# A small transformer on one core: the encoder's residual goes from identity products on TensorE to rows added by VectorE, and maxima products are spread between feed-forward products

## The reference

```python
def layer(h, p):                       # 6 times, on h = x + pos_encoding
    q, k, v = (h @ w + b, split into 16 heads of 8)
    scores = einsum("bhqd,bhkd->bhqk", q, k) / sqrt(8)
    scores = scores * sierpinski_mask
    att = softmax(scores) @ v, merged heads, @ wo + bo
    h = _ln(h + att, g1, be1)
    ff = gelu(h @ w1 + b1) @ w2 + b2   # 128 -> 512 -> 128
    return _ln(h + ff, g2, be2)
```

## Time and profile before

| what | value |
|---|---|
| time, median of 3 runs | 4445.66 us (4441.06 to 4448.02) |
| the profiled execution's time | 4436.53 us |
| its span, first to last instruction | 4434.5 us |
| TensorE busy | 3725.7 us (84%) |
| VectorE busy | 2560.0 us (58%) |
| ScalarE busy | 1880.3 us (42%) |
| GpSimd busy | 783.7 us (18%) |
| mean granted TensorE clock | 0.916 |

### The profile page before, as it was taken

How to read it: one execution, slowest core, us unless ns; L and a number is a source line. 1 busy time by engine, 2 the same in 40 slices (tenths; PEclk the granted TensorE clock), 3 DMA queues, 4 the chain that set the end, 5 groups by cost and what they waited for, 6 DMA issues and landing times. The chain is left out here.

```text
span 4434.5 us, 72029 instructions
## 1 busy us (share of the span) xinstructions
PE 3725.7 (84%) x27991; PEld 2608.3 (59%) x27991; DVE 2560.0 (58%) x6629; ACT 1880.3 (42%) x2957; POOL 783.7 (18%) x1073
## 2 busy tenths in 40 slices
PE   5998998998998998995999987677756666997996
PEld 3766666676666766764777754465635432443664
DVE  4756756756756756755222229888678572113763
ACT  2554564654654654653333335322223122331443
POOL 2223212212222222222000001000010230003321
PEclk8999999999999999997999998799877677997997
DMA  5424414414414514511000000000000000002430
GB/s 130 116 46 106 115 41 111 115 36 118 114 37 113 121 37 104 125 33 44 1 1 1 1 15 1 1 1 1 1 6 1 4 0 27 0 0 75 99 88 24
DMA packets 156743, 222.66 MB, mean 50 GB/s; under 512 B 16158, under 2 KB 136350, under 8 KB 139422
## 3 DMA queue, kind: packets, MB, share of 16 engines
q10 hardware_dynamic: 19656, 107.37, 10.9%
q1 hardware_dynamic: 136750, 110.69, 9.1%
HBM read 154.42 MB, written 60.82 MB: 49 GB/s over the span
## 5 line engine op out<-in xcount | busy, mean ns | idle before, releaser
L755 DVE TENSOR_REDUCE enc_mx<-psum 128x2 f32<-128x512 f32 (+1 forms) x1152 | 750.8, 684 | 261.5 <-PE psum L464 259.4
L900 ACT ACTIVATE enc_e<-psum 128x1024 f32<-128x1024 f32 (+1 forms) x768 | 580.3, 808 | 376.1 <-PE psum L483 309.2
L464 PE MATMUL psum<-enc_ks,enc_qs 80*128 80x128 bf16 (+1 forms) x3072 | 453.5, 252 | 88.6 <-DVE enc_mx L755 71.9
L483 PE MATMUL psum<-enc_qs,enc_ks 83*128 83x256 bf16 (+1 forms) x3072 | 378.4, 248 | 18.9 <-DMA enc_qs<-enc_turned_max 13.3
L464 PEld LDWEIGHTS psum<-enc_ks,enc_qs 80*128 80x128 bf16 x3072 | 216.9, 99 | 223.2 <-DVE enc_mx L755 129.0
L494 PE MATMUL psum<-enc_e,enc_v 128*32 128x256 f32 (+1 forms) x6144 | 329.3, 332 | 0.0
L1775 ACT ACTIVATE moe_act_h<-psum 128x512 f32<-128x512 f32 x288 | 169.4, 598 | 306.8 <-PE psum L1649 306.7
L483 PEld LDWEIGHTS psum<-enc_qs,enc_ks 83*128 83x128 bf16 x3072 | 258.1, 98 | 55.0 <-DMA enc_qs<-enc_turned_max 17.9
L1671 PEld LDWEIGHTS psum<-par_s,moe_act_h 128*128 128x128 f32 x2304 | 269.7, 192 | 30.1 <-issue 28.5
L1671 PE MATMUL psum<-par_s,moe_act_h 128*128 128x128 f32 x2304 | 272.6, 275 | 0.0
L1738 DVE SCALAR_TENSOR_TENSOR moe_acc<-psum,moe_gates,moe_acc 128x128 f32<-128x128 f32 x256 | 72.1, 344 | 345.3 <-PE psum L1671 345.3
(11 more groups left out here) (468 smaller groups left out, 7183.9 us busy)
## 6 DMA issues: line engine op xcount, KB each, us to landing
enc_qs<-q_pieces ACTq DMA_DIRECT2D x234, 192.0 KB
enc_ks<-k_pieces ACTq DMA_DIRECT2D x234, 192.0 KB
k_pieces<-enc_pieces SPq DMA_DIRECT2D x240, 128.0 KB, 2.0
q_pieces<-enc_pieces SPq DMA_DIRECT2D x144, 128.0 KB, 2.1
enc_qs<-q_pieces SPq DMA_DIRECT2D x54, 192.0 KB
enc_ks<-k_pieces SPq DMA_DIRECT2D x54, 192.0 KB
rope_qs<-q_pieces ACTq DMA_DIRECT2D x39, 192.0 KB
rope_ks<-k_pieces ACTq DMA_DIRECT2D x39, 192.0 KB
```

What stands on the lines that cost most here:

```text
L464: last = T_.matmul(p1[f % 2][:, i * kw:(i + 1) * kw], qs[0:KEYED, slot, h, j * P:(j + 1) * P], ks[0:KEYED, slot, h, 0:kw], start=True, sto ...
L483: last = T_.matmul(p2[ch][:, g], ks[0:SCORED, slot, 4 * T + g, ch * P:(ch + 1) * P], qs[0:SCORED, slot, 4 * T + g, 0:n], start=True, stop= ...
L755: V.tensor_reduce(mx[:, u % 2, j * HEADS + h0:j * HEADS + h0 + n], p1[f % 2].rearrange("p (h k) -> p h k", h=n), AX_X, ALU.max)\
L900: A.activation(e_of(T, ch), p2[ch], ACT.Exp, scale=HD ** -0.5).then_inc(s_e, 1)
```

## The change

1. The residual is kept as rows. `res` (one slot for each of the 8 groups) holds what is to be added. After N1's apply of a group GpSimd writes `res = normed * g1 + (be1 + b2)` for the feed-forward (`residual1`, two instructions, L376 and L379 of the kernel after), and after N2's apply `res = normed * g2 + (be2 + bo of the next layer)` for the next layer's attention (`residual2`, L384 and L387). `shifts` makes the two sums of biases once in a layer.
2. VectorE adds `res` to the rows in PSUM and writes `rows` (`add1`, L817, and `add2`, L826), in place of ScalarE's `move`. The identity products, `held` and `hold` are gone.
3. Gains and biases are now wanted as rows on all partitions: `layerr` grows from 128x1162 to 128x1928 words, the constants `s1` by 128 columns. SyncE waits for `residual2` of the last group (`s_res2`) before it loads the next `layerr`.
4. At the start TensorE turns the 8 groups of `H` into rows (32 transposes) and VectorE makes the first `res` with 8 adds.
5. The maxima products of the next layer are put one by one behind each `up` product and behind each tile of `down` from g = 5 on; the last six come after the loop.

```diff
@@ sync, attend
                     sp.wait_ge(N2.s_done, at(layer, GROUPS, 2 * GROUPS))
+                    sp.wait_ge(s_res2, at(layer, GROUPS, 2 * GROUPS))
                     sp.dma_start(LR.sb[:], c.params["layerr"][1:][ds(layer, 1)].rearrange("l p w -> p (l w)")).then_inc(LR.sem, 16)
@@ gpsimd
-            def hold(layer, half, g):
...
-                G.tensor_tensor(held[:, half, g % 2], c.H[:, grp(g)], bias.broadcast_to([P, GROUP]), ALU.add).then_inc(s_held[half], 1)
+            def residual2(layer, g):
+                n = at(layer, GROUPS, g)
+                pool.wait_ge(N2.s_normed, n + 1)
+                G.tensor_tensor(res[:, g], N2.normed[:], LR["g2r"].unsqueeze(1).broadcast_to([P, TILES, D]), ALU.mult).then_inc(s_scaled2, 1)
+                pool.wait_ge(s_scaled2, n + 1)
+                pool.wait_ge(s_shift2, layer + 1)
+                G.tensor_tensor(res[:, g], res[:, g], shift2[:].unsqueeze(1).broadcast_to([P, TILES, D]), ALU.add).then_inc(s_res2, 1)
@@ gpsimd, attend
-                        if m:
-                            hold(layer, 0, m - 1)
+                        if m == 1:
+                            shifts(layer, last)
+                        if m >= 2:
+                            residual1(layer, m - 2)
+                        if u == 0 and layer:
+                            residual2(layer - 1, GROUPS - 1)
...
                 for g in range(GROUPS):
+                    if g >= 2 and not last:
+                        residual2(layer, g - 2)
                     if g:
                         N2.root(pool, at(layer, GROUPS, g - 1))
@@ tensor
-                    T_.matmul(b[:, sl], att_t[:, sl], LR["wo"], start=True, stop=False)
-                    last = T_.matmul(b[:, sl], held[:, 0, g % 2, sl], c.ident, start=False, stop=True)
+                    last = T_.matmul(b[:, sl], att_t[:, sl], LR["wo"], start=True, stop=True)
...
-                    T_.matmul(down_bank[:, sl], held[:, 1, g % 2, sl], c.ident, start=True, stop=False)
...
+                    between(t)
@@ tensor, attend, feed-forward
+                    behind = (lambda f: fill(layer, 1, (g - 5) // 2, 6 * ((g - 5) % 2) + f) if f < 3 else None) if g >= 5 and not last_layer else (lambda f: None)
                     if g + 1 < GROUPS:
-                        up(layer, g + 1)
+                        up(layer, g + 1, behind)
...
-                    down(layer, g)
+                    down(layer, g, among)
@@ vector
+            def add1(layer, g, b):
+                n = at(layer, GROUPS, g)
+                dve.wait_ge(N1.s_rows, n + 1)
+                dve.wait_ge(s_res2, n + 1)
+                if n:
+                    dve.wait_ge(N1.s_normed, n)
+                V.tensor_tensor(N1.rows[:], b.rearrange("p (t d) -> p t d", t=TILES), res[:, g], ALU.add).then_inc(N1.s_moved, 1)
@@ vector, attend
+                        if T == 0 and odd and m:
+                            add1(layer, m - 1, misc)
...
+                    if n and not last:
+                        dve.wait_ge(s_scaled2, n)
...
                     N2.apply(dve, n)
+                    if 1 < g < GROUPS:
+                        add2(layer, g)
```

More of the change, by code:

```diff
@@ L425, in attend @@
                 N2.root(pool, at(layer, GROUPS, GROUPS - 1))
+                if not last:
+                    residual2(layer, GROUPS - 2)
                 if last:
@@ L476, in scores_t @@
                 slot = u % SLOTS
+                if layer == 0 and u == 0 and T == 0 and ch == 0:
+                    pe.wait_ge(s_res2, GROUPS)
                 if T == 0 and ch == 0:
@@ L538, in up, with down @@
                     T_.matmul(up_bank[f], LR["w1"][:, f * P:(f + 1) * P], c.H[:, grp(g)], start=True, stop=True).then_inc(s_h, 1)
-            def down(layer, g):
-                pe.wait_ge(s_held[1], at(layer, GROUPS, g + 1))
+                    between(f)
+            def down(layer, g, between=lambda t: None):
                 if g:
@@ L656, in attend @@
                 for g in range(GROUPS):
+                    behind = (lambda f: fill(layer, 1, (g - 5) // 2, 6 * ((g - 5) % 2) + f) if f < 3 else None) if g >= 5 and not last_layer else (lambda f: None)
                     if g + 1 < GROUPS:
-                        up(layer, g + 1)
+                        up(layer, g + 1, behind)
+                    else:
+                        for f in range(3):
+                            behind(f)
                     if g == 0:
@@ L698, in attend @@
                         close(g)
-                    if 4 <= g and not last_layer:
-                        u, f0 = ((0, 0), (0, 6), (1, 0), (1, 6))[g - 4]
-                        for f in range(f0, f0 + 3):
-                            fill(layer, 1, u, f)
                 if not last_layer:
-                    for f in range(9, 12):
+                    for f in range(6, 12):
                         fill(layer, 1, 1, f)
@@ L721, in _ @@
             project_v(0, 0, 0, bank[0])
+            for g in range(GROUPS):
+                if g >= len(x_banks):
+                    pe.wait_ge(s_res2, g - len(x_banks) + 1)
+                for t in range(TILES):
+                    last = T_.transpose(x_banks[g % len(x_banks)][:, t * P:(t + 1) * P], c.H[:, g * GROUP + t * P:g * GROUP + (t + 1) * P], c.ident)
+                last.then_inc(s_x_rows, 1)
             for u in range(2):
@@ L782, in normalise, with add2 @@
                 V.tensor_tensor(out, num[:, half, :, :, 1:VW], rec[:, half].unsqueeze(3).broadcast_to([P, JT, hh, HD]), ALU.mult).then_inc(s_att, 1)
+            def add1(layer, g, b):
+                n = at(layer, GROUPS, g)
+                dve.wait_ge(N1.s_rows, n + 1)
[3 more added lines that the diff above has]
+                V.tensor_tensor(N1.rows[:], b.rearrange("p (t d) -> p t d", t=TILES), res[:, g], ALU.add).then_inc(N1.s_moved, 1)
+            def add2(layer, g):
+                n = at(layer, GROUPS, g)
+                dve.wait_ge(N2.s_rows, n + 1)
+                dve.wait_ge(s_res1, n + 1)
+                if n:
+                    dve.wait_ge(N2.s_normed, n)
+                V.tensor_tensor(N2.rows[:], down_bank.rearrange("p (t d) -> p t d", t=TILES), res[:, g], ALU.add).then_inc(N2.s_moved, 1)
             def close(k):
@@ L833, in attend @@
                         dve.wait_ge(N2.s_turned, n)
+                    if g == 1:
+                        add2(layer, 0)
                     N2.statistics(dve, n)
                     if g == 1:
+                        add1(layer, GROUPS - 1, bank[1])
                         N1.statistics(dve, at(layer, GROUPS, GROUPS - 1))
@@ L869, in _ @@
             move_v(0, 0, 0, bank[0])
+            for g in range(GROUPS):
+                dve.wait_ge(s_x_rows, g + 1)
+                V.tensor_tensor(res[:, g], x_banks[g % len(x_banks)].rearrange("p (t d) -> p t d", t=TILES),
+                                W["bo0"].unsqueeze(1).broadcast_to([P, TILES, D]), ALU.add).then_inc(s_res2, 1)
             for u in range(2):
@@ L952, in attend @@
                                 act.wait_ge(LR.sem, at(layer, 16, 16))
-                            N1.move(act, at(layer, GROUPS, m - 1), misc)
                         if T == 0 and u:
@@ L975, in attend @@
                         move_att(layer, GROUPS - 1, bank[0])
-                    if g == 1:
-                        N1.move(act, at(layer, GROUPS, GROUPS - 1), bank[1])
                     if g == 3 and not last:
```

69 lines of the change are left out of this document (39 added, 30 removed).

## The result

| | before | changed |
|---|---|---|
| time, median (lowest to highest) | 4446.84 us (4439.24 to 4449.69, 6 runs) | 4428.14 us (4422.73 to 4434.6, 6 runs) |
| ratio to before, 95% interval | | 0.9961 [0.995, 0.9973] |
| profiled execution; its span | 4436.53 us; 4434.5 us | 4428.41 us; 4426.6 us |

The change made the kernel 18.7 us faster (0.4%). The forecast was 58 us faster, and 4428.14 lies just above the upper end of its range.

What follows compares the result with a forecast made beforehand. TensorE was taken to bound attention nearly everywhere, feed-forward less surely. Terms 37 + 45 + 4 - 25 - 3 - 1.5 = 56.5, say 57 us, took the profiled 4436.5 to 4380; 9 us offset gave 4388 us, range 4358 to 4428.

Steps and rivals of the forecast that it cites:

- rival 1: Whole kernel: the gains and losses come as summed, 4388 us, own range 4368 to 4408; chance 0.62.
- Groups 0 to 2: 3.6 us: Feed-forward, not last layer: three down and one set of attention rows save 0.89 us each, 3.6 us a layer.
- Of 0.89 + 1.97 us I keep 0.8: Feed-forward group 4: identity saving and held wait go, but root ends 1.7 us later; 0.8 us a layer gained.
- rival 5: Attention: GpSimd's longer work holds up VectorE's normalising, 2.5 us for each of 42 pairs, 105 us, 4493 us; chance 0.04.
- Groups 5 and 6 and the tail: Feed-forward: groups 5 and 6 gain 2.0 us in all, group 7 and tail 2.5 us (1 to 3), a layer.
- TensorE has a block of value products and a maxima product to do before it wants bank 5 again, which covers it: Attention: VectorE's new add costs nothing; without cover it would cost 42 x 0.75 = 32 us.
- Rival 3: Attention gives nothing back, as VectorE's maxima come late behind the attention rows: + 37, 4425 us; chance 0.08.
- in a stretch without a gap on TensorE: Attention: 7 of 8 groups' rows are made where TensorE never idles, so removing identity products saves 37 us.
- forecast's split: Layer boundary: TensorE's 4.9 us wait for the row of maxima, 3.5 us without the load ahead in the queue.
- 3 us for five boundaries: Layer boundaries: after the new wait the granted clock can be 0.50 for a stretch; 3 us lost (0 to 9).
- The start's term: Kernel start: larger layerr and constants are issued ahead of the bit rows, 1.5 us lost; transposes and adds cost nothing.
- Rival 4: Feed-forward: gain from spacing the maxima products is lost in turn's new wait, 4 us a layer less, 4408 us; chance 0.14.

Runs made afterwards that it cites:

- Experiment 6: experiment 1 with GpSimd's residual1 of group 7 moved ahead of root of group 1 in the feed-forward; 4379.26 us, ratio 0.9864 to before.
- Experiment 7: experiment 1 with residual2 of group 2 between the pieces of groups 0 and 1, and of group 6 ahead of the last root; 4381.76 us.
- experiment 8: experiment 1 with the moves of Experiment 5, Experiment 6 and Experiment 7 together; 4360.55 us, ratio 0.9822 to before.
- experiment 1: The changed kernel with the last group's residual2 issued at the layer's end, not behind the next layer's pieces; 4390.13 us, ratio 0.9893 to before.
- Experiment 5: experiment 1 with VectorE's add1 in odd sequences placed before its second block of maxima, not after; 4377.46 us, ratio 0.9862 to before.
- experiment 2: The changed kernel with SyncE issuing the row of maxima of sequence 1 ahead of the layerr load; 4419.67 us, ratio 0.9952 to before.
- experiment 4: The kernel of before with only the spreading of the feed-forward's maxima products, identity products kept; 4423.55 us, ratio 0.9959 to before.
- Experiments 3: The changed kernel with the feed-forward's maxima products back in blocks of three, so the residual part alone; 4445.05 us, ratio 1.0012 to before.

## Why the prediction was wrong

The mechanisms were those forecast in rival 1; three terms of the sum had the wrong size. The largest miss is the feed-forward's, and its main reason is that I priced the work that GpSimd gets by its duration, but did not place it instruction by instruction.

**Feed-forward, the 16.5 us.** I follow the `turn`s from the layer's first `up`, mean of layers 0 to 4. By the `turn` of group 3 I had the gain at 3.6 + 0.8 = 4.4 us a layer; it was 1.1 (56.7 → 55.6). From there to the last `turn` I had 4.5 and it was 3.9 (98.0 → 92.9 for the last, in all 5.0). So the failed step is "Groups 0 to 2: 3.6 us", with "Of 0.89 + 1.97 us I keep 0.8".
- The `turn` of group 0 came 2.7 us earlier, as three times 0.89; that of group 1 only 1.2, since it now waits 2.12 us where it didn't wait before, and that of group 2 only 0.9. The earlier trace rows had shown that GpSimd's full tensors stretch `apply`, and I used it for the old pieces and for rival 5, but not for the new `residual1` of group 7, which the order puts right behind `root` of group 1. Experiment 6 moves it: that `turn` comes at 29.2 in place of 30.6, 2.6 us earlier than before's.
- Group 3: `root` behind `residual2` of group 2 was foreseen, and its price too low. Experiment 7 takes it away: the `turn` comes 2.5 us earlier on average.
- With all moves the `turn` of group 3 comes 5.7 us earlier than before's and the last 8.9 us. The 9 us a layer were there to be had; the change's order didn't give them. (The five feed-forwards have 19 us less at half clock in experiment 8 than in the changed kernel, so a part of the last 3.8 us a layer is clock.)

**Groups 5 and 6 and the tail.** From the `turn` of group 3 to that of group 5 the stretch fell from 22.4 to 20.4 us, the 2.0 of the sum; the predicted wait of the `turn` is there, 1.0 and 1.2 us in place of 1.3. From there to the last `turn` it fell from 18.9 to 17.0, so 1.9 and not 2.5. The last `apply` beside `residual2` of group 6 takes 1.1 us more than alone; with experiment 7, which moves that residual, this stretch is 16.0 us, against 16.9 in experiment 1.

**Attention, 8 us.** "TensorE has a block of value products and a maxima product to do before it wants bank 5 again, which covers it" is the failed sentence. The add takes 0.68 us (0.75 forecast) but starts up to half a microsecond late behind two maxima, so 36 of the 42 odd sequences got 0.5 us on average, mostly 0.55, and not 0.89: 19 us in place of 32. Experiment 5 brings most of them to 0.89. Rival 3's mechanism was real, at a fifth of its price (6.8 us). The other six, the last of each layer, got 2.3 us each, 8.6 us that no term of the sum has: "in a stretch without a gap on TensorE" didn't hold there, where `turn` waited 1.24 us before. So that attention gives 37.6 us with experiment 5, against a forecast 37, is in part luck: the extra 8.6 us stand against sequences that still got less than 0.89 or even lost a little.

**The boundary, 10 us.** The wait itself was close: 5.84 us against 4.9, and 28.0 us more waiting for rows in all against 24.5. In the forecast's split (3.5, the load's issue included, and 1.4) the first part was 3.2 us and the load's transfer 2.7: the load landed 4.8 us after its issue, where I took 4.3, and the row was used only 1.0 us after that, where I let both land together. By the Trainium skill's rule of ring order that stood beside the sum (page "DMA: Bandwidth & Descriptors", section "Queues, rings and completion order"), the row goes behind the load: experiment 2 agrees, 5.4 us from issue to use behind the load and 2.8 ahead of it. The under-sized term is the clock. I had 3 us for five boundaries; 38.2 - 28.0 = 10.2 us are left beside the wait. The half-clock time in sequences 0 and 1 of the six layers went from 33.6 to 79.5 us, and fell back to 36.5 with the wait in experiment 1. In layers 1 to 5 the same 285 or so TensorE instructions of these two sequences, none of them an identity product, kept the engine busy for 146.6 us in place of 130.6.

**What held.** GpSimd's pair 1.27 + 1.27 us; VectorE's add at 0.68 and 0.69 us; the load issued 14 us later; the wait of maxima products gone from the iterations of groups 5 and 6, though not from the tail (3.0 us a layer in place of 7.4, so "nearly gone" was too much). The last feed-forward gave 6.2 (4 forecast). The start's term was of the right sign: the first scores come 3.1 us later (70.6 against 67.5 us), with 2.5 us more for the bit rows; in experiment 4, which has before's start, they come at 68.9, so about half of it can be scatter. Layer 0's first two sequences took 3.6 back; they had 11.5 us at half clock before and 4.2 in the changed kernel.

**Rival 4** (a growing wait for `turn`) was half right: the wait for `apply` rose by 42 us, though mainly from GpSimd's place and not from the spacing. With the spreading alone it is 67.5 us against 54.7; the rest of the rise belongs to the residual part or to both together, and the moves of GpSimd's instructions take 24 us of it away (experiment 8). **Rival 5** had its mechanism in the trace after all, once a layer, below. Experiments 3 and 4 show what no rival of mine said: as ordered, the residual part was worth nothing, and spreading all.

**The range.** Attention, the feed-forward's 5 us a layer and the wait each lay within their own bounds, and the clock just beyond (10.2 against at most 9). The upper end was reckoned wrongly as well: 5 us a layer in feed-forward with 6.5 us a boundary is 4388 + 20 + 7.5 = 4415.5 us and not 4428, and rival 3 gives 4425. The range had room for one or two of these misses and not for three together: 8.0 + 19.7 + 10.2 us short, less 4 us by which the last layer and the start did better. They had a common cause in part: where GpSimd's new work stands. The feed-forwards had more half clock too (51.0 us in five, against 39.4 before); what that cost isn't separated.

## What to carry to other kernels

When work moves to an engine that runs in order, write down for each new instruction what it stands in front of and what runs beside it on the neighbour engine; here four pairs of a layer in the wrong place, and one add behind two maxima, cost 68 us with the clock that went with them (4428 against 4361; 62 by the ratios to before), more than the whole change gave. A load that must wait for the last reader of its buffer belongs where that reader is early, and never ahead of a small transfer that is needed at once. A wait costs more than its length where the clock falls in it. When a change has two parts, time each alone: the sum hid that one was worth nothing, and that moving one call makes it worth some 33 us (4390 against 4424 for the other part alone).

## What the runs showed of the hardware

VectorE and GpSimd, all instructions of the changed kernel's encoder. The multiplication L808 (two SBUF tensors) took 0.29 us in 186 of 192 cases and 1.15 to 1.16 us in six, once a layer, always when it began some 0.27 us behind L379 of GpSimd; it ends 0.15 us after it:

```profile
294.42 1.28 POOL L379 TENSOR_TENSOR enc_res<-enc_res,enc_shift 128x512 f32<-128x512 f32 x1
...
294.68 1.16 DVE L808 TENSOR_TENSOR enc_att<-enc_num,enc_rec 128x128 f32<-128x128 f32 x1
```

Where L808 began first (30 times ahead of L347), it kept its 0.29 us. In the earlier trace rows no such case occurs. This is what the Trainium skill, page "SBUF — State Buffer", section "Who interferes with whom", states: an instruction of VectorE with two SBUF inputs contends with GpSimd's reads, and the first to issue has the shared port for the whole instruction while the other is blocked. The trace agrees, but for the 0.15 us where 0.29 would be a whole L808. It cost VectorE 5 us in all; whether TensorE waited for any of it I did not follow. The paragraph on rival 5 called `apply` a case of this rule. It isn't one by that sentence, as it reads one full SBUF tensor and scalars; what the runs show of it is its length beside GpSimd.

The adds from PSUM and `res` were never stretched: L826 took 0.69 us in the 20 cases beside a GpSimd tensor operation and 0.69 in the 28 without. The maxima (PSUM alone) took 0.68 us in 325 cases beside one and in 827 without. Those slowed were all SBUF to SBUF, one of the four of an `apply` from 0.34 to at most 1.42 us and the small L172 from 0.17 to 0.73 us at most, but not every such one was: the statistics on L161 took 0.28 us beside a GpSimd operation and without.

The clock at a boundary: in each of the five waits of 5.7 to 6.2 us TensorE's granted clock fell to 1.2 GHz 2.0 to 2.3 us after the wait began, and stayed there for 6.2 to 6.8 us beyond its end; in experiment 2 it fell in the five waits of 2.7 to 2.8 us too. The same work took longer in it: a row of value products on L522 1.51 us against 0.86. With the short wait there is less of it in sequences 0 and 1, but not none: 32 to 37 us in experiments 1, 5 and 6, and 54 and 60 in 7 and 8, where the wait for the row is as short. Why one boundary has it and another not stays open.
